# An attention layer and a routed expert layer on one core: smaller last tiles, expert tables in pieces, earlier first products, weights in pieces

## The chip, the cores and the metric

The kernel runs on one core of one Trainium2 chip. The metric is the device time of one execution in microseconds, as the median of several runs. The engines are called as in the profile: PE (TensorE), PEld (its weight loads), DVE (VectorE), ACT (ScalarE), POOL (GpSimd), SP (SyncE).

## The reference

The input is x, 16 sequences of 512 tokens with 128 features, in 32-bit floats. What is computed:

```python
def _layernorm(x, axis=-1, eps=1e-05): ...
# attention, 16 heads of 8
scores = jnp.einsum('bhqd,bhkd->bhqk', Q, K) / jnp.sqrt(jnp.float32(dk))
probs = jax.nn.softmax(scores, axis=-1)
intervened = probs.at[:, :, :, 0].set(0.0)
intervened = intervened / jnp.clip(intervened.sum(axis=-1, keepdims=True), 1e-09, None)
combined = probs + LAMBDA * (intervened - probs)      # LAMBDA = 0.5
x = _layernorm(x + (combined @ V) @ Wo.T + bo)
# experts: each token goes to the best two of 8, weighed by phi_routing
for e in range(E):
    h = jax.nn.silu(x @ w1[e].T) * (x @ w3[e].T)      # 128 -> 512
    out = out + wte[:, e:e + 1] * (h @ w2[e].T)       # 512 -> 128
x = _layernorm(x + out)
```

## The kernel before

**Attention.** The work is cut into 64 units (16 sequences of 4 groups of 4 heads), and the whole program into periods of one unit, from -12 to 63, each of 8 steps. Every engine runs the same list of periods by itself, and semaphores tie them together. In period p the scores and exponentials of unit p are computed (lines 472 and 635), the row maxima of unit p+2 (461 and 769), and the products with the values of unit p-1 (484). The products for q, k and v of a later sequence, the output product and the routing products stand at fixed steps between them: the table `BEHIND` at line 240. So that q and k can be multiplied in bf16, each is split into three bf16 parts by `split_qk` on POOL (1096 to 1109: copy, subtract, copy, subtract). SP stores the parts in DRAM (`store_parts`, 316) and `load_qk` (324) loads them into four large buffers, `regions`, in six transfers for each unit.

**Start.** SP issues wq, wk, bq, bk, then the first xT, then wv, gate, four pieces of wo, bv and bo (300 to 309). All twelve weights count on one semaphore, and PE (527), ACT (624) wait for all of it ahead of their first work. DVE first fills the rows 64 to 127 of two regions with ones (752), then sets the constants of its own (753 to 760).

**Routing.** When a sequence is through the first layer norm, DVE works out its two experts and the places of its rows in six parts (`route`, 828), POOL counts (`count_rows`, 1177) and scatters 1,024 rows of 132 words to `rows_d` in DRAM, expert by expert (`scatter`, 1192: two choices of four indirect DMAs). A row holds the token, its number and its weight.

**Experts.** `rows_d` is read in tiles of 256 rows of one expert. There are 71 (`TILES`, 43): 64 full ones' worth of rows and up to 7 more because each expert's last tile is part empty. The first 45 (`FIRST`) come from the first 13 sequences (`ROUTED`), which are scattered when the tiles start. The tables of a tile's expert and first row are worked out on DVE in two lots (`first_tables` at 941, and `rest_by_expert`, `rest_by_tile` at tiles 11 and 12). What is left of attention and routing for the last three sequences is done among the first 13 tiles: the functions `tail` of DVE and POOL, `TAIL_RING` of PE and ACT.

A tile t runs so. SP loads its rows into one of 6 buffers (410 to 413; the buffer is free when the result of tile t-6 was scattered). PE transposes (`tile_in`, 547), ACT copies the transposed rows out (706) and the two expert weights into fixed buffers (`copy_weights`, 695, two copies of 128x512 whatever the tile's size). PE makes up (560), ACT its silu (721), PE lin (569), DVE their product (1037), PE down (585), DVE scales by the row's weight (1031), POOL adds the rows to `x1_d` or `y_d` in DRAM in turn, 128 rows for each indirect DMA (1272). The order on PE is the loop at line 600:

```python
tile_up(t); beside(t, 0); tile_in(t + 1); tile_down(t - 1); tile_lin(t); beside(t, 1)
```

The sums up and lin have one buffer each: `tile_up` waits for the silu of the tile before, `tile_lin` for the product of the tile before. The weights W1 and W3 (2 MB each) are loaded in one transfer each in period 61 (362 to 365) into regions that attention no longer needs, and W2 ahead of the row load of tile 6 (397 to 399).

**Order at the seam.** SP loads the rows of tile 0 when 13 sequences are scattered (392 to 394). POOL scatters sequence 13 behind the row load of tile 0 (1240 to 1242, `pool.wait_ge(*rows_in(0))`), sequence 14 at tiles 6 and 7, sequence 15 at tiles 11 and 12.

**Final stage.** Five buffers, the sum of `x1_d` and `y_d` on PE (617), statistics on DVE, the factors on POOL, the normalisation on ACT.

## Time and profile before

| what | value |
|---|---|
| median of 3 runs | 1364.8 us (1364.0 to 1367.9) |
| the profiled execution's own time | 1357.14 us |
| its span from the first to the last instruction | 1355.4 us |
| mean granted clock of TensorE | 0.981 of 2.4 GHz |
| busy: PE, DVE, ACT, POOL | 1272.2, 941.3, 822.7, 725.4 us |
| attention, up to the first up product of the experts | 0 to 891.4 us |
| tiles, from the first to the last up product | 891.4 to 1294.1 us |
| final stage, from its first load | 1309.6 to the end |

How the rows are read. In the windows a row gives the stretch and its length, then the busy time of PE, PEld, DVE, ACT and POOL with their instructions in brackets, the granted clock of TensorE (1.00 is 2.4 GHz, 0.50 is 1.2 GHz), the busy share of the DMA engines and GB/s. In a timeline a row gives the start, how long it took, engine, line and operation, what it writes and reads, the count, and in brackets how long the engine idled before it and what released it; "SPq" is the queue of SP, and several merged operations are one row. In the chain of waits a row gives the start, the length and the work; it is the chain that is followed back from the last instruction. Buffers that are used twice have the name of the first owner: `probs_sb` are also the tile's silu, product and result, `values_sb` are also the rows of a tile, `k_parts_sb` the transposed rows, `xT_sb`, `full_q_sb` and `full_k_sb` the copied expert weights. fp32 matmuls are two records each.

### The profile page before, as it was taken

How to read it: one execution, taken by the hardware profiler on the slowest of the kernel's cores; microseconds unless marked ns; L12 is line 12 of the kernel's file. 1: busy time of each engine (PE TensorE's matmuls, PEld its weight loads, DVE VectorE, ACT ScalarE, POOL GpSimd, SP SyncE). 2: the span in 40 equal slices, each digit the busy share in tenths (PEclk: the TensorE clock that was granted, in tenths of full speed). 3: DMA queues.
4: the chain of work that ended last, by engine and by line, in shares of the span. 5: the costliest groups of instructions: out<-in, count | busy, mean ns of one | idle time of the engine just before them, and what ended most of it. 6: DMA issues, size and time to landing. Idle time of an engine off the chain costs nothing.

```text
span 1355.4 us, 22134 instructions
## 1 busy us (share of the span) xinstructions
PE 1272.2 (94%) x7214; PEld 657.1 (48%) x7214; DVE 941.3 (69%) x1560; ACT 822.7 (61%) x1587; POOL 725.4 (54%) x913
## 2 busy tenths in 40 slices
PE   2799999999999999999999999998899999999967
PEld 1133333333333333333333333257789999999942
DVE  6788898898899898988988999833533333333324
ACT  1277777777777777777777777763434444444416
POOL 4324254474474564654644733546775555555547
PEclk8699999999999999999999999999999999999979
DMA  3322323233323323233232231443344333333327
GB/s 102 121 87 67 94 70 98 80 94 93 95 82 94 109 71 105 84 94 91 88 97 81 84 95 33 152 131 54 59 73 69 53 51 48 48 49 46 43 94 279
DMA packets 111888, 117.18 MB, mean 86 GB/s; under 512 B 17440, under 2 KB 91680, under 8 KB 111392
## 3 DMA queue, kind: packets, MB, share of 16 engines
q1 hardware_dynamic: 86960, 97.62, 23.5%
q0 software_dynamic: 24816, 18.15, 9.2%
q8 instruction: 60, 0.98, 0.3%
q14 instruction: 52, 0.43, 0.1%
HBM read 70.81 MB, written 45.29 MB: 86 GB/s over the span
## 4 chain that ended last, share of the span: by engine, by line
PE 72%; DVE 16%; issue 4%; POOL 3%; DMA 2%; ACT 1%; SPq 1%; another core or an unknown queue 0%; POOLq 0%; ACTq 0%; DVEq 0%
PE acc_ps L484 15%; PE ring_ps L472 13%; PE mx_ps L461 12%; DVE rowmax_sb L769 10%; PE ring_ps L585 8%; PE mx_ps L569 8%; PE mx_ps L560 8%; PE ring_ps L504 1%; PE ring_ps L501 1%; PE ring_ps L499 1%; PE ring_ps L509 1%; POOL x_d L1272 1%; PE ring_ps L518 1%; PE ring_ps L550 1%; DVE TN_sb L778 1%
## 5 line engine op out<-in xcount | busy, mean ns | idle before, releaser
L769 DVE TENSOR_REDUCE rowmax_sb<-mx_ps 128x2 f32<-128x1024 f32 x512 | 607.0, 1213 | 88.3 <-PE mx_ps L461 82.9
L635 ACT ACTIVATE probs_sb<-ring_ps 128x512 f32<-128x512 f32 x1024 | 558.7, 598 | 103.9 <-PE ring_ps L472 88.8
L472 PE MATMUL ring_ps<-region_sb 74*128 74x512 bf16 x1024 | 356.8, 381 | 3.7 <-ACT prefix_sb L671 2.1
L461 PE MATMUL mx_ps<-region_sb 72*128 72x512 bf16 x1024 | 310.3, 385 | 11.1 <-DVE rowmax_sb L769 5.2
L484 PE MATMUL acc_ps<-probs_sb,values_sb 128*32 128x512 f32 x2048 | 272.6, 605 | 5.4 <-DVE TN_sb L778 5.4
L472 PEld LDWEIGHTS ring_ps<-region_sb 74*128 74x128 bf16 x1024 | 100.9, 99 | 234.7 <-ACT probs_sb L635 131.8
L702 ACT ACTIVATE xT_sb<-region_sb 128x512 f32 x71 | 44.8, 630 | 207.4 <-PE mx_ps L569 187.8
L1091 POOL CAST negmax_parts_sb<-negmax_sb 16x128 bf16<-16x128 f32 x64 | 17.9, 280 | 274.9 <-ACT negmax_sb L641 274.9
L1272 POOL DMA_INDIRECT x_d<-probs_sb,values_sb x72 | 111.9, 1554 | 87.4 <-DVE probs_sb L1031 66.5
L461 PEld LDWEIGHTS mx_ps<-region_sb 72*128 72x128 bf16 x1024 | 95.7, 99 | 123.7 <-DVE rowmax_sb L769 36.1
L1031 DVE TENSOR_SCALAR probs_sb<-ring_ps,values_sb 128x128 f32<-128x128 f32 x142 | 43.2, 346 | 159.6 <-PE ring_ps L585 146.0
L1196 POOL DMA_INDIRECT rows_d<-sent_sb,pos_sb x128 | 126.2, 986 | 48.4 <-issue 43.7
L585 PE MATMUL ring_ps<-region_sb,probs_sb 128*128 x1136 | 139.4, 276 | 10.1 <-DVE probs_sb L1037 9.9
L1272 POOL DMA_INDIRECT y_d<-probs_sb,values_sb x70 | 108.7, 1553 | 72.9 <-DVE probs_sb L1031 59.8
L1037 DVE TENSOR_TENSOR probs_sb<-mx_ps,probs_sb 128x1024 f32<-128x1024 f32 x71 | 86.9, 1224 | 79.9 <-PE mx_ps L569 76.1
L560 PE MATMUL mx_ps<-k_parts_sb,xT_sb 128*128 128x256 f32 x568 | 135.9, 383 | 2.8 <-issue 2.8
L585 PEld LDWEIGHTS ring_ps<-region_sb,probs_sb 128*128 128x128 f32 x1136 | 132.4, 192 | 12.6 <-issue 12.4
L560 PEld LDWEIGHTS mx_ps<-k_parts_sb,xT_sb 128*128 128x128 f32 x568 | 108.3, 191 | 18.6 <-issue 3.9
L484 PEld LDWEIGHTS acc_ps<-probs_sb,values_sb 128*32 128x32 f32 x2048 | 40.5, 108 | 113.3 <-issue 94.4
L721 ACT ACTIVATE probs_sb<-mx_ps 128x1024 f32<-128x1024 f32 x71 | 72.6, 1022 | 9.2 <-PE mx_ps L560 6.6
L569 PE MATMUL mx_ps<-k_parts_sb,full_q_sb 128*128 128x256 f32 x288 | 68.1, 379 | 0.0
L569 PE MATMUL mx_ps<-k_parts_sb,full_k_sb 128*128 128x256 f32 x280 | 66.2, 379 | 0.0
(150 smaller groups left out, 1206.0 us busy)
## 6 DMA issues: line engine op xcount, KB each, us to landing
region_sb<-parts_d SPq DMA_DIRECT2D x384, 96.0 KB
values_sb<-rows_d SPq DMA_DIRECT2D x71, 132.0 KB
parts_d<-q_parts_sb SPq DMA_DIRECT2D x16, 384.0 KB, 2.6
parts_d<-k_parts_sb SPq DMA_DIRECT2D x16, 384.0 KB, 2.9
xT_sb<-xT SPq DMA_DIRECT2D x16, 256.0 KB, 3.1
x_sb<-x SPq DMA_DIRECT2D x16, 256.0 KB
x_d<-xn_sb SPq DMA_DIRECT2D x16, 256.0 KB
y_d<-padrow_sb SPq DMA_DIRECT2D x16, 256.0 KB
```

What stands on the lines that cost most here:

```text
L461: last = nc.tensor.matmul(mx_ps[n % 2][:, i, :], QS[b % 2][0:KR, h, P * c:P * (c + 1)], KS[b % 2][0:KR, h, :], start=True, stop=True)
L472: nc.tensor.matmul(bank, KS[b % 2][0:KR + MR, h, P * c:P * (c + 1)], QS[b % 2][0:KR + MR, h, :], start=True, stop=True).then_inc(s_ring_re ...
L484: last = nc.tensor.matmul(acc_ps[VW * j:VW * (j + 1), 0, :], VE[b % 2][:, c, HG * g + j, :], PT[u % 2][:, j, c, :], start=(c == 0), stop=( ...
L560: last = nc.tensor.matmul(up_ps[:, c, :], W1T[t % 2][:, P * c:P * (c + 1)], XGT[t % 2], start=True, stop=True)
L569: last = nc.tensor.matmul(lin_ps[:, c, :], W3T[t % 2][:, P * c:P * (c + 1)], XGT[t % 2], start=True, stop=True)
L585: last = nc.tensor.matmul(y_ps[:, at:at + D], HH[t % 2][:, c, P * w:P * (w + 1)], W2[:, bass.ds(expert + c * D, D)], start=(c == 0), stop= ...
L635: nc.scalar.activation(PT[u % 2][:, i // QC, i % QC, :], ring_bank("st", u, i), ACT.Exp, scale=SCALE).then_inc(s_ring_done, 1)
L721: nc.scalar.activation(SG[t % 2], up_ps, ACT.Silu).then_inc(s_silu, 1)
L769: V.tensor_reduce(rowmax[u % 2][:, 2 * k:2 * k + 2], mx_ps[n % 2][:, :, :], axis=AXX, op=ALU.max, negate=True).then_inc(s_mx_done, 1)
L1037: V.tensor_tensor(HH[t % 2], lin_ps, SG[t % 2], ALU.mult).then_inc(s_h, 1)
L1196: G.indirect_dma_start(rows_d, bass.IndirectOffsetOnAxis(ap=pos[b % 2][:, s, c:c + 1], axis=0), XE[b % 2][:, c, s, :], None).then_inc(s_sc ...
L1272: G.indirect_dma_start((x1_d, y_d)[t % 2], bass.IndirectOffsetOnAxis(ap=XG[t % RING][:, w, D:D + 1].bitcast(i32), axis=0), YO[t % YRING][: ...
```

## The change

1. A tile is full (256 rows) or half (128 rows). 57 full ones come first, then 21 halves, 78 in all. Every operation of a half tile has half its columns, but for the two weight copies. A half tile has one scatter-add instead of two.
2. The tables are worked out for the full tiles among the rows known at first (45), for 12 more full ones, and for the halves, the latter two in six pieces at tiles 15 to 27. The running sum over experts has three additions instead of seven.
3. POOL scatters sequence 13 in period 63, behind `send_x` of sequence 14, and no longer waits for rows. SP's first row load waits until 14 sequences are scattered. Sequence 14 is scattered in twos at tiles 6 to 9, sequence 15 at tiles 13 to 16. Step 5 of sequence 14's routing moves from tile 3 to behind the layer norm of tile 5, steps 4 and 5 of sequence 15 to tiles 10 and 12.
4. xT of the first sequence is issued first; the first products wait for wq, wk, bq and bk alone; v, the halved wo and the rest wait for the other eight.
5. The first k is split on DVE, beside POOL's split of q. The rows of ones are written as 32-bit words that hold two bf16 ones (64x4096 instead of 64x8192), one region before that split and one behind it, and a unit's load waits for its own region only.
6. W1, W3 and W2 are loaded in quarters, each when the unit that held its place is through: W1 and W3 in periods 57 to 60, W2 in 61 to 63 and ahead of tile 6's rows.

The core of the diff:

```diff
-TILES = 2 * NT // TK + E - 1
+FULL = 2 * NT // TK - (E - 1)
+TILES = FULL + (2 * NT - FULL * TK) // P + E - 1
...
+        def split_done(b, which):
+            return (s_k0_split, 1) if (b, which) == (0, 1) else (s_split, split_no(b, which) + 1)
+        def halves(t):
+            return HALVES if t < FULL else 1
...
+            load_xT(0)
             for dst, src in ((wq_sb, wqT), (wk_sb, wkT), (bq_sb, bq), (bk_sb, bk)):
-                sp.dma_start(dst[:, :], src).then_inc(s_weights, 16)
-            load_xT(0)
+                sp.dma_start(dst[:, :], src).then_inc(s_weights_qk, 16)
...
-                    sp.wait_ge(s_ones, 2)
+                    sp.wait_ge(s_ones, b % 2 + 1)
...
+            def load_weights(u, s_loaded, *weights):
+                sp.wait_ge(s_ring_ready, ring_at["st", u, 15] + 1)
+                words = slice(E * F // NG * (u % NG), E * F // NG * (u % NG + 1))
+                for dst, src in weights:
+                    sp.dma_start(dst[:, words], src[:, words]).then_inc(s_loaded, 16)
...
-                if p == UNITS - NG + 1:
-                    sp.wait_ge(s_ring_ready, ring_at["st", UNITS - NG - 1, 15] + 1)
-                    for dst, src in ((W1, w1T), (W3, w3T)):
-                        sp.dma_start(dst[:, :], src).then_inc(s_w13, 16)
...
+                if UNITS - 2 * NG < p <= UNITS - NG:
+                    load_weights(p - 1, s_w13, (W1, w1T), (W3, w3T))
+                elif p > UNITS - NG:
+                    load_weights(p - 1, s_w2, (W2, w2T))
...
-            sp.wait_ge(s_scattered, SPARE + SENT * ROUTED)
+            sp.wait_ge(s_scattered, SPARE + SENT * (ROUTED + 1))
...
-            pe.wait_ge(s_weights, s_weights_last)
-            pe.wait_ge(s_const, 6)
+            pe.wait_ge(s_weights_qk, s_weights_qk_last)
...
                 for c in range(FC):
-                    last = nc.tensor.matmul(up_ps[:, c, :], W1T[t % 2][:, P * c:P * (c + 1)], XGT[t % 2],
+                    n = P * halves(t)
+                    last = nc.tensor.matmul(up_ps[:, c, 0:n], W1T[t % 2][:, P * c:P * (c + 1)], XGT[t % 2][:, 0:n],
                                             start=True, stop=True)
...
-            for n in range(2):
-                V.memset(KS[n][64:P, :, :], 1.0).then_inc(s_ones, 1)
-            dve.wait_ge(s_const, 6)
+            two_ones = float(np.array([0x3F803F80], np.uint32).view(np.float32)[0])
+            V.memset(regions[2][64:P, :], two_ones).then_inc(s_ones, 1)
+            dve.wait_ge(s_ring_done, ring_at["k", 0] + 1)
+            exact, parts = full[1], qk_parts[1]
+            V.tensor_copy(parts[:, 0, :], exact[:, :]).then_inc(s_k0_step, 1)
+            dve.wait_ge(s_k0_step, 1)
+            V.tensor_tensor(exact[:, :], exact[:, :], parts[:, 0, :], ALU.subtract).then_inc(s_k0_step, 1)
...
+            V.tensor_tensor(parts[:, 2, :], exact[:, :], parts[:, 1, :], ALU.subtract).then_inc(s_k0_split, 1)
+            V.memset(regions[3][64:P, :], two_ones).then_inc(s_ones, 1)
+            dve.wait_ge(s_const, 1)
...
-                elif t == 3:
-                    route(NB - 2, 5)
...
                 elif t == 5:
                     ln_apply(NB - 1)
+                    route(NB - 2, 5)
...
-                elif t in (9, 10):
-                    route(NB - 1, t - 5)
-                elif t == 11:
+                elif t == 10:
+                    route(NB - 1, 4)
+                elif t == 12:
+                    route(NB - 1, 5)
+                elif t == 13:
                     V.tensor_copy(end_i[:, :], offs[0:1, QC, :]).then_inc(s_ends, 1)
+                elif t == 15:
+                    full_by_expert()
...
                 if g == 3:
                     if is_seq(b - 1):
                         send_x(b - 1)
+                    if b == NB - 1:
+                        for s in range(2):
+                            scatter(b - 2, s)
...
                 if t == 0:
-                    pool.wait_ge(*rows_in(0))
-                    for s in range(2):
-                        scatter(b - 2, s)
                     add_bo(b)
...
-                elif t in (6, 7):
-                    scatter(b - 1, t - 6)
-                elif t == 9:
-                    count_rows(b)
-                elif t in (11, 12):
-                    scatter(b, t - 11)
+                elif t in (6, 7, 8, 9):
+                    if t == 9:
+                        count_rows(b)
+                    scatter(b - 1, (t - 6) // 2, range(t % 2 * 2, t % 2 * 2 + 2))
+                elif t in (13, 14, 15, 16):
+                    scatter(b, (t - 13) // 2, range((t - 13) % 2 * 2, (t - 13) % 2 * 2 + 2))
...
-                for w in range(HALVES):
+                for w in range(halves(t)):
                     G.indirect_dma_start((x1_d, y_d)[t % 2], bass.IndirectOffsetOnAxis(
```

## Rows read from the trace of the kernel before

**Rows 1.** Windows: the first tile and 100 us of steady tiles.

```profile
892.00:896.00 4.00, 4.00 (x19) 2.13 (x21) 1.09 (x6) 2.08 (x3) 3.38 (x4) 0.58 0.94 365
1150.00:1250.00 100.00, 100.00 (x622) 91.39 (x622) 33.64 (x56) 43.34 (x72) 55.76 (x36) 1.00 0.35 47
```

**Rows 2.** Chain of waits over one steady tile: start us, us, what.

```profile
1201.22 1.73 PE mx_ps L560 x8
...
1203.16 1.79 PE ring_ps L585 x16
1204.95 1.73 PE mx_ps L569 x8
```

**Rows 3.** Chain of waits of the first 60 us, the pieces that hold it.

```profile
8.23 5.51 DMA bo_sb<-bo
...
14.18 2.06 PE ring_ps L499 x2
...
24.50 2.83 DMA parts_d<-k_parts_sb
...
45.16 4.47 DMA xT_sb<-xT
```

**Rows 4.** Timeline of the first 45 us: start us, us long, engine line op.

```profile
2.58 6.88 DVE L752 MEMSET region_sb<- 64x8192 bf16 x1 [2.58 <-issue]
2.67 0.43 SPq L298 DMA_DIRECT2D xT_sb<-xT  x1
...
17.97 0.69 ACT L650 ACTIVATE full_k_sb<-ring_ps,bk_sb 128x512 f32<-128x512 f32 x1 [1.02 <-PE ring_ps L501]
...
19.63 1.15 POOL L1109 TENSOR_TENSOR q_parts_sb<-full_q_sb,q_parts_sb 128x512 bf16<-128x512 f32 x1
...
35.02 11.68 DVE L769 TENSOR_REDUCE rowmax_sb<-mx_ps 128x2 f32<-128x1024 f32 x10 [8.19 <-PE mx_ps L461]
```

**Rows 5.** Line 298 in the first 10 us.

```profile
DMA to landing us min/median/max: 2.9/2.9/2.9
```

**Rows 6.** Timeline from the last attention unit to the first tile.

```profile
881.06 0.25 POOL L1175 TENSOR_SCALAR dest_sb<-dest_sb 128x8 f32<-128x8 f32 x1
...
882.65 6.77 SPq L412 DMA_DIRECT2D values_sb<-rows_d  x6
...
885.18 1.09 POOL L1196 DMA_INDIRECT rows_d<-sent_sb,pos_sb  x1 [3.87 <-DMA values_sb<-rows_d]
...
891.44 3.35 PE L560 MATMUL mx_ps<-k_parts_sb,xT_sb 128*128 128x256 f32 x8 [2.78 <-issue]
...
894.19 0.95 POOL L1196 DMA_INDIRECT rows_d<-sent_sb,pos_sb  x1 [0.30 <-issue]
```

**Rows 7.** Timeline of a steady tile on ACT, DVE and POOL.

```profile
1201.32 1.22 DVE L1037 TENSOR_TENSOR probs_sb<-mx_ps,probs_sb 128x1024 f32<-128x1024 f32 x1 [1.19 <-PE mx_ps L569]
...
1201.87 0.63 ACT L702 ACTIVATE xT_sb<-region_sb 128x512 f32 x1 [3.05 <-PE mx_ps L569]
...
1202.98 1.02 ACT L721 ACTIVATE probs_sb<-mx_ps 128x1024 f32<-128x1024 f32 x1
...
1203.90 0.38 ACT L706 ACTIVATE k_parts_sb<-ring_ps 128x256 f32<-128x256 f32 x1
...
1206.36 1.55 POOL L1272 DMA_INDIRECT x_d<-probs_sb,values_sb  x1 [2.06 <-DVE probs_sb L1031]
```

**Rows 8.** Timeline of two tiles late behind counts, and a late signal.

```profile
920.06 0.19 DVE L888 TENSOR_TENSOR place_sb<-prefix_sb,offs_sb 128x32 f32<-128x32 f32 x1 [4.44 <-POOL offs_sb L1190]
...
922.55 2.05 PE L585 MATMUL ring_ps<-region_sb,probs_sb 128*128 x16 [1.08 <-DVE probs_sb L1037]
...
961.83 0.61 DVE L1031 TENSOR_SCALAR probs_sb<-ring_ps,values_sb 128x128 f32<-128x128 f32 x2 [4.38 <-remote]
```

**Rows 9.** Chain of waits from the last tile to the final stage.

```profile
1294.05 1.73 PE mx_ps L560 x8
...
1306.78 2.71 DMA x_d<-probs_sb,values_sb
```

More of the change, by code:

```diff
@@ L280, in rows_out @@
         def rows_out(t):
-            return s_y_out[t % YRING], 16 * HALVES * (t // YRING + 1)
+            return s_y_out[t % YRING], 16 * sum(halves(n) for n in range(t % YRING, t + 1, YRING))
         def is_tile(t):
@@ L568, in tile_lin @@
                 for c in range(FC):
-                    last = nc.tensor.matmul(lin_ps[:, c, :], W3T[t % 2][:, P * c:P * (c + 1)], XGT[t % 2],
+                    n = P * halves(t)
+                    last = nc.tensor.matmul(lin_ps[:, c, 0:n], W3T[t % 2][:, P * c:P * (c + 1)], XGT[t % 2][:, 0:n],
                                             start=True, stop=True)
@@ L581, in tile_down @@
                     pe.wait_ge(s_y, t - 1)
-                for w in range(HALVES):
+                for w in range(halves(t)):
                     at = TK * (t % 2) + D * w
@@ L623, in _ @@
         def _(act):
[L624 to L625 removed]
+            act.wait_ge(s_weights_qk, s_weights_qk_last)
             def ring_bank(*what):
@@ L901, in tb, with whole_tiles, tile_places @@
                 dve.wait_ge(s_tab, step_of_tab[0])
[L903 removed]
+            cnt, tiles, cum, taken, move, upto, start = (tabc[:, n, :] for n in range(7))
             tile_no, expert, row0, woff = (tab[:, n, :] for n in range(4))
[L906 removed]
+            def whole_tiles(n, rows):
                 tb(V.tensor_copy(tabi[:, :], n))
[L908 removed]
+                tb(V.tensor_scalar(tabi[:, :], tabi[:, :], rows.bit_length() - 1, None, ALU.logical_shift_right))
                 tb(V.tensor_copy(tiles, tabi[:, :]))
             def running_sum():
[L912 to L916 removed]
+                of, into = padded[:, 0, :], padded[:, 1, :]
+                tb(V.tensor_copy(of[:, E:2 * E], tiles))
+                for shift in (1, 2):
+                    tb(V.tensor_tensor(into[:, E:2 * E], of[:, E:2 * E], of[:, E - shift:2 * E - shift], ALU.add))
+                    of, into = into, of
+                tb(V.tensor_tensor(cum, of[:, E:2 * E], of[:, E - 4:2 * E - 4], ALU.add))
+            def tile_places(first, last):
                 ge, gn = tile_by_expert(first, last)
@@ L924, in by_tile @@
                     return x.unsqueeze(1).to_broadcast([1, last - first, E])
+                tb(V.tensor_scalar(move, tiles, -1.0, None, ALU.mult))
+                tb(V.tensor_tensor(move, move, start, ALU.subtract))
+                tb(V.tensor_tensor(move[:, 0:E - 1], move[:, 0:E - 1], start[:, 1:E], ALU.add))
                 tb(V.tensor_tensor(ge, tile_no[:, 0:last - first].unsqueeze(2).to_broadcast([1, last - first, E]),
@@ L930, in tile_table, with tile_rows @@
                 tb(V.tensor_reduce(no, gn, axis=AXX, op=ALU.add))
+            def tile_rows(first, last, rows):
+                which = slice(first, last)
+                no = tab[:, 4, 0:last - first]
                 tb(V.tensor_tensor(no, tile_no[:, 0:last - first], no, ALU.add))
-                if first > 0:
-                    tb(V.tensor_tensor(no, no, taken[:, 0:1].to_broadcast([1, last - first]), ALU.add))
+                tb(V.tensor_tensor(no, no, start[:, 0:1].to_broadcast([1, last - first]), ALU.add))
                 tb(V.tensor_scalar(row0[:, which], expert[:, which], float(REGION), None, ALU.mult))
-                tb(V.scalar_tensor_tensor(out=row0[:, which], in0=no, scalar=float(TK), in1=row0[:, which],
+                tb(V.scalar_tensor_tensor(out=row0[:, which], in0=no, scalar=float(rows), in1=row0[:, which],
                                           op0=ALU.mult, op1=ALU.add))
@@ L1028, in _ @@
                         dve.wait_ge(*rows_out(t - 1 - YRING))
-                    for w in range(HALVES):
+                    for w in range(halves(t - 1)):
                         at = TK * ((t - 1) % 2) + D * w
@@ L1270, in _ @@
                     pool.wait_ge(*rows_out(t - 2))
-                for w in range(HALVES):
+                for w in range(halves(t)):
                     G.indirect_dma_start((x1_d, y_d)[t % 2], bass.IndirectOffsetOnAxis(
```

123 lines of the change are left out of this document (74 added, 49 removed).

## The prediction

> **What bounds the kernel now.** I read the profile in five steps. First the busy shares and the 40 slices: TensorE is at nine tenths nearly everywhere, so the question is which waits remain at the seams and what TensorE does in the expert stage. Second, the windows: in 100 us of steady tiles PE is busy for all 100, at full clock, while ACT has 43, DVE 34 and POOL 56 [rows 1]. Only fewer PE columns make this stage shorter. Third, the chain of waits over one steady tile: up 1.73 us, two transposes in a gap of 0.21, down 1.79, lin 1.73, 5.46 us in all, with nothing but PE in it [rows 2]. Fourth, the chain of the first 60 us. The first product starts at 14.18, when the last weight (bo) has landed, though it uses neither bo, wo nor wv. Behind it lie product, bias, both splits one after the other on POOL, the store of k at 24.50 and its landing, then a row of loads issued by SP; the load of the third xT (45.16) still ends a wait [rows 3]. So this stretch is a chain, and what leaves it shifts all of attention. Fifth, the seam to the experts and the end [rows 6, 8, 9]. The first up starts at 891.44 and the last at 1294.05 [rows 6, 9]: 402.6 us for 70 tiles, where 70 x 5.46 is 382.2. Some 20 us are lost among the first sixteen tiles.
>
> **Part 1, the first products.** Before, the xT load was issued fifth, at 2.67, and landed 2.9 later [rows 4, 5], at 5.6. Now xT goes first and the four small loads end in that place; I take the same 5.6 for the last of them, so the first product starts 14.18 - 5.6 = 8.6 us earlier. Lower bound of the gain 7.5 (four loads behind a 256 KB one), upper 9.2. The k split moves from POOL, where it stood behind the q split (ended 20.78) [rows 4], to DVE. k leaves ACT at 18.66, that is 4.5 after the product's start [rows 4]. Four DVE operations on 128x512: the only row of such work is 1.22 us for 1024 elements [rows 7], so 0.65 each, 2.6 together. k can be stored 7.1 after the product's start instead of 24.50 - 14.18 = 10.3: 3.2 us more. The q split (6.6 after the start) stays just ahead of it. I give back 0.5 us because the remaining weights (landed 13.74 [rows 3]) now share the queues with the stores. Sum: -11.3 us; ends -8 (DVE and POOL slow each other) and -13. Cover: the DVE memset of 6.88 writes words instead of halves, half as many elements, 3.4 us; the second one now follows the split, until 16.2. The constants took from 18.0 to 26.8 on DVE [rows 4], 8.8 us, so they end near 25.0, while the first maxima could start at 35.02 - 11.3 = 23.7. They are 1.3 us late, but ten of them ended at 46.7 [rows 4] and the next waited for xT until 49.63 [rows 3]: 2.9 us of cover. The late constants cost nothing; without the cover they would cost 1.3.
>
> **Part 2, expert weights in pieces.** The same bytes are issued in the last seven periods behind the move of the row maxima; each period lasts 10 us or more. In the trace nothing waits for W1 or W3, and the first down follows the second up without a gap. I take 0, between -1 (a lighter W2 load; the DMA share was 0.94 under it [rows 1]) and +3 (the loads of q, k and maxima queue behind a piece).
>
> **Part 3, the new wait ahead of the first tile.** This is the part that speaks against the change. SP issued the first row load at 882.65, when 13 sequences were scattered; the fourteenth was scattered from 885.18 on, after that load had landed 2.5 us later, and its eight scatters took until 895.1 [rows 6], a pitch of 1.29 us. Now POOL begins them when it has sent the fifteenth sequence, at 881.3, and SP waits for all of them ahead of its first load. Last scatter done: 881.3 + 0.4 + 7 x 1.29 + 0.95 = 891.7. Landing: the nearest row has 2.71 for a scatter-add [rows 9]; a plain one I take at 2.0. Register read and issue 0.5, load 2.5, transposes and copy 0.9: the first up starts at 897.6 instead of 891.44, +6.2 us. Queued behind SP's wait are the other five row loads (1.35 each) and the last quarter of W2; the second down needs it only some 9 us later. PE has nothing else in its order. The clock: behind a wait of 2.78 us the granted clock was 0.58 over 892 to 896, the 1.2 GHz level for most of it, and the first up took 3.35 instead of 1.73 [rows 1, 6, 2]. After a wait of 9 us I expect at least the same and half as much again: +0.8. Sum +7.0, ends +3 and +10. The Trainium skill ("TensorE: Matmul & The Clock Gate", section "HAM oscillation") says that a wait for DMA lets the gate fall so that the following work starts cold; it speaks against this part, and this trace agrees for the short wait with the 3.35 us.
>
> **Part 4, the tail of attention among the tiles.** The part of routing that needs POOL's counts now stands three or more tiles behind them. DVE waited 4.44 us for the counts and down stood 1.08 [rows 8]; a second such place, three sequences' scatters later, cost as much. Against that, POOL does its work in nearly the same order and route step 5 now lies behind the layer norm. Three signals of PE came late while scatters were in flight (one DVE wait of 4.38 with an unknown releaser [rows 8]); scatters in twos may or may not calm that. Tables in pieces of at most some ten small operations fit in DVE's 66 idle us of 100 [rows 1]: 0. Sum -3, ends 0 and -8.
>
> **Part 5, 57 full and 21 half tiles for 71.** No pass is lost: eight experts leave less than one full tile each, so 57 full ones always exist. Down already has 128 columns: 1.79 / 16 = 0.112 per matmul, against 1.73 / 8 = 0.216 for 256 columns [rows 2]. A half tile is 24 x 0.112 + 0.11 = 2.80 us of PE. ACT doesn't halve: its weight copies begin 0.65 after the last lin and take 1.11, then half of silu 0.51 and of the copy 0.25: 2.52 [rows 7]. DVE: 0.1 + 0.65 until down may start, under the 1.0 of up and transpose. POOL: one scatter-add of 1.55 and about 0.8 of lead [rows 7]. PE stays the bound with 0.3 us to spare; I take 2.85. So 14 x 5.46 = 76.4 is exchanged for 21 x 2.85 = 59.9: -16.5 us. Ends: -17.6 (2.80) and -5 (3.4: ACT's silu and copy don't shrink, 3.06, and 0.3 of semaphores).
>
> **Part 6, the last tile.** Behind the last lin half of the multiply (-0.6), of down (-0.9), of the scaling (-0.3) and one scatter-add with its lead (-1.85) go: -3.6; ends -2.5 and -4.5. The final stage is unchanged.
>
> **Sum.** -11.3 + 0 + 7.0 - 3.0 - 16.5 - 3.6 = -27.4. The profiled execution took 1357.1: 1329.7. The median of the runs shown, 1364.8, lies 7.7 above it; I keep that distance: 1337. A measurement of this kernel can tell some 0.3% (4 us) from no change.
>
> **Rivals.**
> *Half tiles keep their fixed parts.* A slot falls to 3.6 us instead of 2.85, since the copies, semaphores and the single-buffered sums stay as they are. For it: ACT is only 0.3 us shorter than PE. Against: DVE and ACT idle for more than half of a full tile. 21 x 3.6 = 75.6: part 5 gives 0.8, the total -11.7, 1353. Chance 0.16. The Trainium skill ("VectorE: DVE Perf Modes", section on the TRN2 errata) has SBUF-source operations pay a fixed latency each and advises 512 elements or more; that speaks for this rival. The slots here keep 512 elements except the copy of 128, and no row of before shows that one.
> *The seam costs little and the late signals go.* Part 3 at +3, part 4 at -8: -36.4, 1328. Chance 0.12.
> *Slower: the ring of row buffers.* A tile's rows are loaded when the scatter of six tiles before has landed; if load, scatter-add and landing keep the full tile's time, the half tiles go at the pace of that loop. By rows it is 3 (read, issue, load) + 2 slots and 1.25 + 0.8 + 1.55 + 2.71 = 15 us for six, 2.5 per tile, under 2.85. It decides from 4.2 per tile: (76.4 + 10.9) / 21. At 4.6 the time is +9.3, 1374. Chance 0.05.
>
> **How the numbers follow.** The forecast has 0.67: 1337, its own range 1326 to 1347. Rivals 0.16, 0.12, 0.05. The range from 1320 to 1355 holds forecast, both faster rivals and the ends of parts 1 and 3; the slower rival is left out. Faster by over 4 us: 0.93; within: 0.03; slower: 0.04.
>
> **What would show it.** First product near 5.6 and k stored near 12.7; first maxima around 25; first up near 897.6 with the clock at half behind it; half tiles of 2.85 in the chain with PE alone; the last scatter issued 3.6 nearer to the last lin. Wrong would be: ACT or DVE in the chain of the half tiles, first up before 893, a wait for xT that doesn't move.

## The result and the profile after

Four executions of the changed kernel took 1332.5 to 1347.9 us, median 1344.5; the kernel before took 1364.4 beside it (1351.8 to 1367.9). The ratio is 0.9868, with an interval from 0.9828 to 0.9908: 18 us faster, between 12.6 and 23.5. The forecast was 1337 us and 27.4 us faster. Executions of one kernel spread by some 10 us or more, so the runs below are compared by their ratios and milestones.

The profiled execution took 1345.6 us, span 1343.7, against a span of 1355.4: 11.7 us shorter. Where these went, from one milestone to the next (the forecast of +7.0 has 6.2 for the wait up to the first up and 0.8 for the lower clock behind it):

| stretch | before | after | difference | forecast |
|---|---|---|---|---|
| start to last exponential of attention | 887.5 | 889.55 | +2.05 | -11.3 |
| from there to the first up | 3.94 | 11.46 | +7.5 | +7.0 |
| first up to the 58th up | 331.5 | 323.4 | -8.1 | -3.0 |
| 14 full tiles, or 21 half ones | 76.45 | 64.1 | -12.4 | -16.5 |
| last slot's end to first final load | 10.3 | 6.6 | -3.7 | -3.6 |
| final stage | 45.8 | 48.7 | +2.9 | 0 |

**The start.** The chain of waits of the changed kernel answers to [rows 3] (start us, us, what):

```profile
2.67 2.41 DMA bk_sb<-bk
5.12 2.09 PE ring_ps L521 x2
7.28 1.28 ACT L677
8.58 0.69 ACT full_q_sb L677
9.27 0.59 ACT full_k_sb L677
...
14.19 3.46 DMA parts_d<-k_parts_sb
17.72 0.70 SPq L354
...
35.48 4.96 DMA xT_sb<-xT
```

The first product starts at 5.12 instead of 14.18, k is stored at 14.19 instead of 24.50, SP issues the first of the row of q and k loads at 17.72 instead of 27.40, and xT at 35.48 instead of 45.16: from the loads on the chain lies 9.7 us earlier. Between 17.72 and 35.48 nothing but SP's own issuing holds it, some 0.7 us for each of 24 loads and 0.45 for each of two stores. The timeline of the two splits, to be read beside [rows 4]:

```profile
9.34 0.61 POOL L1177 CAST q_parts_sb<-full_q_sb 128x512 bf16<-128x512 f32 x1 [3.63 <-ACT full_q_sb L677]
...
10.04 1.28 POOL L1179 TENSOR_TENSOR full_q_sb<-full_q_sb,q_parts_sb 128x512 f32<-128x512 f32 x1
10.34 1.52 DVE L789 TENSOR_TENSOR full_k_sb<-full_k_sb,k_parts_sb 128x512 f32<-128x512 f32 x1
...
12.64 1.52 DVE L793 TENSOR_TENSOR k_parts_sb<-full_k_sb,k_parts_sb 128x512 bf16<-128x512 f32 x1
...
27.64 9.42 DVE L811 TENSOR_REDUCE rowmax_sb<-mx_ps 128x2 f32<-128x1024 f32 x8
```

The subtractions took 1.52 us each on DVE, the whole split 4.3. Both end 0.54 us behind the subtraction of POOL that was under way when they began (11.32 and 13.62 on POOL, 11.86 and 14.16 on DVE). PE began the products for the first maxima at 24.20; DVE takes the maxima at 27.64, 0.03 behind the last of its constants.

Then the 9.7 us are lost again, and the windows show to what (us, busy time and count of PE, PEld, DVE, ACT, POOL, granted clock, DMA share, GB/s):

```profile
30.00:50.00 20.00, 16.31 (x31) 3.81 (x32) 14.57 (x14) 1.64 (x3) 1.81 (x5) 0.50 0.48 149
50.00:100.00 50.00, 49.96 (x196) 16.37 (x195) 34.38 (x31) 30.62 (x59) 12.00 (x19) 0.71 0.20 62
```

The same two windows of the kernel before:

```profile
30.00:50.00 20.00, 11.72 (x33) 3.27 (x32) 11.68 (x10) 2.24 (x4) 10.00 (x13) 0.67 0.52 163
50.00:100.00 50.00, 48.27 (x224) 15.02 (x225) 40.66 (x36) 33.35 (x64) 12.02 (x19) 0.91 0.27 82
```

PE is busy for nearly all of the 50 us in both (49.96, and 48.27 before), but at a granted clock of 0.71 instead of 0.91 it got through 196 matmuls instead of 224. TensorE had 1.2 GHz, half of 2.4, from 27.8 to 79.0 here, and before from 21.5 to 31.7 and from 38.6 to 59.1. Unit 2's maxima start at 52.0 (before 61.0), unit 4's at 84.6 (82.5), unit 12's at 188.1 (186.0).

**The seam.** POOL's and PE's timeline, which answer to [rows 6]:

```profile
885.13 1.09 POOL L1270 DMA_INDIRECT rows_d<-sent_sb,pos_sb  x1 [0.46 <-issue]
...
894.13 0.96 POOL L1270 DMA_INDIRECT rows_d<-sent_sb,pos_sb  x1 [0.30 <-issue]
```

```profile
899.82 0.66 PE L576 MATMUL ring_ps<-ident_sb,values_sb 128*128 128x128 f32 x2 [9.47 <-DMA values_sb<-rows_d]
901.01 2.50 PE L587 MATMUL mx_ps<-k_parts_sb,xT_sb 128*128 128x256 f32 x5 [0.53 <-ACT k_parts_sb L736]
```

SP issues nothing more from 885.2 until the last of the eight scatters has landed, and issues the first row load at 897.42. PE waits 9.47 us.

**The half tiles.** The chain of one of them, beside [rows 2]:

```profile
1252.85 0.89 PE mx_ps L587 x8
1253.74 0.11 PE ring_ps L576
1253.85 1.09 PE ring_ps L613 x8
1254.94 0.89 PE mx_ps L597 x8
```

That is up, transpose, down and lin: 2.98 us, PE alone. Down has the same count of columns as up and lin and takes 0.2 more.

### The profile page after: what moved, and what is told of

It reads as the page before. It is cut to its first block, busy times and chain, and to the rows that moved or that the text cites. A ratio compares the mean times of both kernels' runs of the same rounds, so it can differ in the third digit from the quotient of the medians.

```text
span 1343.7 us, 22455 instructions
## 1 busy us (share of the span) xinstructions
PE 1274.6 (95%) x7263; PEld 654.0 (49%) x7263; DVE 940.4 (70%) x1591; ACT 830.0 (62%) x1615; POOL 712.2 (53%) x902
## 4 chain that ended last, share of the span: by engine, by line
PE 71%; DVE 20%; issue 2%; DMA 2%; POOL 2%; SPq 2%; ACT 0%; DVEq 0%; POOLq 0%; ACTq 0%
PE acc_ps L506 13%; DVE rowmax_sb L811 12%; PE mx_ps L483 12%; PE ring_ps L494 11%; PE ring_ps L613 9%; PE mx_ps L587 8%; PE mx_ps L597 8%; DVE TN_sb L820 2%; PE mx_ps L645 1%; PE ring_ps L529 1%; PE ring_ps L523 1%; PE ring_ps L521 1%; PE ring_ps L576 1%; PE ring_ps L545 1%; DVE stats_sb L843 1%
## 5 line engine op out<-in xcount | busy, mean ns | idle before, releaser
L494 PE MATMUL ring_ps<-region_sb 74*128 74x512 bf16 x1024 | 361.5, 388 | 1.5 <-ACT probs_sb L662 1.4
L483 PE MATMUL mx_ps<-region_sb 72*128 72x512 bf16 x1024 | 317.8, 393 | 11.5 <-DVE rowmax_sb L811 8.7
L731 ACT ACTIVATE xT_sb<-region_sb 128x512 f32 x78 | 49.1, 630 | 188.1 <-PE mx_ps L597 186.8
L1346 POOL DMA_INDIRECT x_d<-probs_sb,values_sb x68 | 106.1, 1561 | 89.6 <-DVE probs_sb L1103 64.8
L1270 POOL DMA_INDIRECT rows_d<-sent_sb,pos_sb x128 | 126.4, 987 | 48.1 <-issue 47.2
L1110 DVE TENSOR_TENSOR probs_sb<-mx_ps,probs_sb 128x1024 f32<-128x1024 f32 (+1 forms) x78 | 84.3, 1080 | 91.5 <-PE mx_ps L597 91.5
L587 PE MATMUL mx_ps<-k_parts_sb,xT_sb 128*128 128x256 f32 (+1 forms) x624 | 132.2, 355 | 0.5 <-ACT k_parts_sb L736 0.5
L613 PEld LDWEIGHTS ring_ps<-region_sb,probs_sb 128*128 128x128 f32 x1080 | 127.9, 193 | 7.8 <-issue 7.7
L752 ACT ACTIVATE probs_sb<-mx_ps 128x1024 f32<-128x1024 f32 (+1 forms) x78 | 70.4, 903 | 4.6 <-PE mx_ps L587 4.6
L597 PE MATMUL mx_ps<-k_parts_sb,full_q_sb 128*128 128x256 f32 (+1 forms) x312 | 65.4, 353 | 0.0
L597 PE MATMUL mx_ps<-k_parts_sb,full_k_sb 128*128 128x256 f32 (+1 forms) x312 | 65.0, 351 | 0.0
```

Of the source, the lines that this page charges most:

```text
L483: last = nc.tensor.matmul(mx_ps[n % 2][:, i, :], QS[b % 2][0:KR, h, P * c:P * (c + 1)], KS[b % 2][0:KR, h, :], start=True, stop=True)
L494: nc.tensor.matmul(bank, KS[b % 2][0:KR + MR, h, P * c:P * (c + 1)], QS[b % 2][0:KR + MR, h, :], start=True, stop=True).then_inc(s_ring_re ...
L587: last = nc.tensor.matmul(up_ps[:, c, 0:n], W1T[t % 2][:, P * c:P * (c + 1)], XGT[t % 2][:, 0:n], start=True, stop=True)
L597: last = nc.tensor.matmul(lin_ps[:, c, 0:n], W3T[t % 2][:, P * c:P * (c + 1)], XGT[t % 2][:, 0:n], start=True, stop=True)
L613: last = nc.tensor.matmul(y_ps[:, at:at + D], HH[t % 2][:, c, P * w:P * (w + 1)], W2[:, bass.ds(expert + c * D, D)], start=(c == 0), stop= ...
L752: nc.scalar.activation(SG[t % 2][:, :, 0:n], up_ps[:, :, 0:n], ACT.Silu).then_inc(s_silu, 1)
```

## The experiments

Ratios are to the kernel before, timed on the same chip beside each. The milestone "unit 12" is the start of its first maxima: 188.1 us in the profile after.

**The old start.** The loads of weights in their old order, the first products waiting for all twelve, k split on POOL; everything else as changed.

```diff
-            load_xT(0)
             for dst, src in ((wq_sb, wqT), (wk_sb, wkT), (bq_sb, bq), (bk_sb, bk)):
...
+            load_xT(0)
...
             pe.wait_ge(s_weights_qk, s_weights_qk_last)
+            pe.wait_ge(s_weights, s_weights_last)
...
-            V.tensor_copy(parts[:, 0, :], exact[:, :]).then_inc(s_k0_step, 1)
...
-                    if is_seq(b + 2) and b + 2 > 0:
+                    if is_seq(b + 2):
```

> The changed kernel with the old start: the small loads ahead of xT, all twelve weights waited for, the first k split on POOL behind q. Theory (the clock took the gain): the first product starts near 14 and the first maxima near 36 again, some 9 us later, but TensorE's granted clock is back at 2.4 GHz some 20 us sooner than in the changed kernel (59 instead of 79), so the last exponential of attention is where it was, within 3 us, and the time is that of the changed kernel within 4 us. Rival (the gain is real and the changed kernel's profile was unlucky): 9 to 11 us slower than the changed kernel. A second rival (the late constants on DVE hold the first units): the same time as the theory, but with the clock as in the changed kernel.

Measured: median 1349.8 of ten, 0.9941 [0.9908, 0.9975], 0.73% above the changed kernel's ratio (10 us; the two intervals touch). In its profile the first product starts at 13.26 and the first maxima at 35.4; the clock was at half from 19.9 to 33.5 and from 36.9 to 81.3, and unit 12 starts at 194.5, 6.4 later than in the profile after. The theory missed: the clock didn't come back sooner (81.3, not 59), and the time isn't the same. The rival's 9 to 11 us fit. So the new start is worth about what the chain says, some 6 to 10 us, and the loss in the profile after isn't its doing alone.

**Filler.** 27 matmuls more (54 records) in the first 42 us, in places where PE would wait; they multiply what is there, and nobody reads their sums.

```diff
+            def filler(count, rhs):
+                for _ in range(count):
+                    nc.tensor.matmul(acc_ps[:, 0, 0:rhs.shape[-1]], wk_sb[:, :], rhs, start=True, stop=True)
...
+                if (name, b) == ("q", 1):
+                    filler(10, xT_sb[0][:, :])
+                elif (name, b) == ("q", 2):
+                    filler(4, xT_sb[1][:, :])
...
+                        if p == -2 and k == 0:
+                            filler(5, xT_sb[1][:, :])
                         maxima(p + 2, k)
+                        if p == -2:
+                            filler(1, xT_sb[1][:, 0:256])
```

> The changed kernel with extra matmuls on PE between the first products and the first units, into a bank that nothing reads before it is started anew: ten of 512 columns ahead of the second q, five ahead of the first maxima, four ahead of the third q, one of 256 columns behind each step of the first maxima. The output is unchanged. Theory (the half clock from 27.8 to 79.0 us takes the gain of the start): the clock stays at or near 2.4 GHz through the first units, unit 3's maxima come less than 13 us behind unit 2's, the last exponential comes at 874 to 880 instead of 889.6, the time is 9 to 15 us below the changed kernel's. Rival (loads and DVE hold the first units whatever the clock): no gain, or up to 5 us slower by the extra work.

Measured: median 1332.8 of six, 0.9834 [0.9796, 0.9871]. Windows of this kernel:

```profile
30.00:50.00 20.00, 17.21 (x55) 7.30 (x54) 16.12 (x15) 2.35 (x5) 1.57 (x4) 0.91 0.48 155
50.00:100.00 50.00, 49.26 (x261) 15.64 (x260) 42.18 (x39) 39.55 (x78) 12.71 (x21) 1.00 0.23 72
```

261 matmuls in the 50 us instead of 196; unit 4 at 71.5 instead of 84.6, unit 12 at 175.0 instead of 188.1. The last exponential comes at 874.6, in the range that the theory gave. So 13 us of the profiled execution were the clock's. But the interval of the ratio overlaps the changed kernel's, so the timed executions don't show that the filler gains.

**Own semaphore.** Sequence 13's scatters count on a semaphore of their own, and SP's first row load waits for 13 sequences again; the waits that need the fourteenth name the new one.

```diff
+        s_scattered_13 = sem("scattered_13")
...
-            sp.wait_ge(s_scattered, SPARE + SENT * (ROUTED + 1))
+            wait_scattered(sp, ROUTED)
...
-                                         XE[b % 2][:, c, s, :], None).then_inc(s_scattered, 16)
+                                         XE[b % 2][:, c, s, :], None)\
+                     .then_inc(s_scattered_13 if b == ROUTED else s_scattered, 16)
```

> The changed kernel with a semaphore of its own for the scatters of sequence 13, so that SP's first row load waits for 13 sequences again while POOL scatters sequence 13 beside it. Theory (the count waits for a sequence that the first tiles don't need): the first row load is issued near 885 instead of 897.4, first up between 891 and 894 instead of 901.0, 7 to 10 us below the changed kernel. Rival (the loads stand behind the scatters' traffic or late row tables): under 4 us.

Measured: median 1328.6 of six, 0.9797 [0.9754, 0.984], 0.71% below the changed kernel's ratio (10 us; the intervals overlap a little). SP's and PE's timeline:

```profile
876.00 6.68 SPq L441 DMA_DIRECT2D values_sb<-rows_d  x6
...
879.73 0.20 PEld L583 LDWEIGHTS ring_ps<-ident_sb,values_sb 128*128 128x128 f32 x2 [0.84 <-issue]
...
881.25 1.99 PE L594 MATMUL mx_ps<-k_parts_sb,xT_sb 128*128 128x256 f32 x8 [1.07 <-ACT k_parts_sb L743]
```

From the last exponential (879.01) to the first up it is 2.24 us instead of 11.46, and the first up takes 1.99 instead of 3.78, with no stretch of the clock at half behind the seam. Up to here the gain is 9.2 us, and the next seventeen tiles are no longer for it (103.2 against 105.1). The theory holds in its difference; its milestones (first up at 891 to 894) took attention's end from the profile after, and here it lies 10.5 earlier. The program's first 180 us are those of the changed kernel, and yet unit 12 starts at 176.5, with 1.2 GHz from 12.6 to 22.8 and from 26.2 to 50.1.

**All tiles full.** 71 tiles of 256 tokens with everything else of the change.

```diff
-TILES = FULL + (2 * NT - FULL * TK) // P + E - 1
+TILES = 2 * NT // TK + E - 1
...
-            return HALVES if t < FULL else 1
+            return HALVES
```

> The changed kernel with 71 full tiles (14 in place of the 21 halves), tables in the same pieces. By the two profiles the half tiles took 64.1 us for 76.4 and the end behind the last slot 6.6 for 10.3: theory 16 us slower than the changed kernel. Rival (part of the saving is the earlier relief of other queues, or a luckier execution): under 10 us.

Measured: median 1355.6 of ten, 0.9989 [0.996, 1.0018]. From the 58th up to the first final load it is 86.0 us, where the half tiles take 70.6: 15.4, as the theory had it. Without the half tiles the rest of the change is worth nothing that can be measured (between 2 us slower and 5 us faster), although by the profiles start, seam, tail and final stage sum to some 8 us less than before (-10 + 7.5 - 8.1 + 2.9) where the clock behind the start takes one of its shorter courses. The mean granted clock of its ten executions is lower, 0.970 in the median for 0.977 of the kernel before beside them. That fits a loss to the clock in the timed executions too; it isn't shown further. Its final stage takes 48.6 us too.

**The changed kernel again**, beside the next three.

> The changed kernel itself once more, unchanged, beside the others on one chip, for a base and to see how its executions spread. Theory (the granted clock in the first 100 us has two courses, and an execution takes one or the other): the executions fall into two groups some 8 to 12 us apart, the slower one with a mean granted clock lower by 0.008 or more; this profile reaches unit 12's maxima either near 176 or near 188 us. Rival (the spread is noise of the whole program): no gap between groups, and no tie to the clock.

Measured: median 1345.7 of six (1341.7 to 1352.4), 0.9863 [0.9814, 0.9912]. Unit 12 starts at 182.0, with 1.2 GHz from 27.4 to 44.5 and from 51.3 to 68.4: a third course of the clock, of the same instructions. The theory of two courses missed: the six don't fall into two groups (five lie between 1341.7 and 1347.6), and the slowest, 1352.4, had a mean clock of 0.968, where four of the others had 0.966 to 0.970.

**Three repairs at once.** The own semaphore; DVE's product in two operations, each tied to half of lin and half of down; and one activation of a single column ahead of ACT's first wait, so that the function table is loaded there.

```diff
-                pe.wait_ge(s_h, t + 1)
+                pe.wait_ge(s_h, 2 * t + 1)
...
+                        if (w, c) == (0, 2):
+                            pe.wait_ge(s_h, 2 * t + 2)
...
-                    V.tensor_tensor(HH[t % 2][:, :, 0:n], lin_ps[:, :, 0:n], SG[t % 2][:, :, 0:n], ALU.mult)\
-                     .then_inc(s_h, 1)
+                    for i in range(2):
+                        dve.wait_ge(s_lin, 2 * t + i + 1)
+                        cs = slice(2 * i, 2 * i + 2)
+                        V.tensor_tensor(HH[t % 2][:, cs, 0:n], lin_ps[:, cs, 0:n], SG[t % 2][:, cs, 0:n], ALU.mult)\
+                         .then_inc(s_h, 1)
...
+            act.wait_ge(s_pool_const, 1)
+            nc.scalar.activation(first_use[:, :], ones[:, 0:1], ACT.Identity)
             act.wait_ge(s_weights_qk, s_weights_qk_last)
```

> The kernel with the semaphore of its own for sequence 13, and in addition DVE's product of a tile in two operations (columns c 0 and 1, then 2 and 3), each tied to its half of lin and of down, and a first activation on ACT ahead of its wait for the weights, so that the function table is loaded early. Theory (in a half tile down waits for the product, and its first weight load isn't hidden: 0.2 us per half tile): half slots of 2.79 to 2.85 us instead of 2.98, full slots 5.46 as before; the table load of 1.28 leaves the start, k is stored 1.3 us earlier. Together 4 to 5.5 us below the kernel with the semaphore alone, at like clock. Rival (the half slot is bound by the 2.52 us of ACT and the semaphores): half slots stay at 2.95 or more.

Measured: median 1324.4 of six, 0.9711 [0.966, 0.9761], the best of all: 1.5% below the changed kernel beside it. Four of the six took 1323.3 to 1324.9 us at a mean clock of 0.979 to 0.983, two 1334.0 and 1335.4 at 0.968 and 0.971. The chain of a half tile:

```profile
1256.48 0.11 PE ring_ps L584
1256.59 0.89 PE ring_ps L624 x8
1257.48 0.89 PE mx_ps L605 x8
1258.38 0.89 PE mx_ps L595 x8
```

Down takes 0.89, the slot 2.79 instead of 2.98, as the theory had it. The table's load no longer stands in the chain: ACT took k 0.35 earlier (8.81 for 9.16), q 1.4 earlier, and k is stored at 13.11 instead of 14.19. PE begins the products for the first maxima 1.1 earlier, but DVE's constants hold the maxima until 27.05, only 0.6 earlier. Two of DVE's operations on k, now beside other operations of POOL:

```profile
10.09 0.98 DVE L802 TENSOR_TENSOR full_k_sb<-full_k_sb,k_parts_sb 128x512 f32<-128x512 f32 x1
11.10 1.26 DVE L804 CAST k_parts_sb<-full_k_sb 128x512 bf16<-128x512 f32 x1
```

The profile holds one of the longer courses of the clock (half from 23.4 to 74.6). Its seam is 5.8 us, not the 2.24 of the version with the semaphore alone, for ACT got the signal for the first tile's rows late, from a sender that the trace doesn't name, while scatters were in flight:

```profile
897.04 0.38 ACT L749 ACTIVATE k_parts_sb<-ring_ps 128x256 f32<-128x256 f32 x1 [3.76 <-remote]
```

**Scatters in fours.**

```diff
-                elif t in (6, 7, 8, 9):
...
+                elif t in (6, 7):
+                    scatter(b - 1, t - 6)
...
+                elif t in (13, 14):
+                    scatter(b, t - 13)
```

> The changed kernel with the scatters of sequences 14 and 15 in fours at tiles 6, 7, 13 and 14 instead of in twos at eight tiles. Theory (the scatters in bursts of four on POOL push the scatter-adds back, and late signals come with them): from the first up to the 18th takes 109 us or more instead of 105.1, 3 to 7 us slower than the changed kernel. Rival (what went is the wait for POOL's counts on DVE alone): 105 to 107 us, time within 2 us of the changed kernel.

Measured: median 1345.4 of four, 0.9872 [0.9804, 0.994]. The first seventeen slots take 108.8 us where the profile after has 105.1 and the changed kernel again 104.7. Totals of waits over this stretch (engine line waited for: us in total, times, longest), first of the kernel before, then of this one; the changed kernel has no such line:

```profile
DVE probs_sb L1031 <- remote: 13.6, 3, 5.0
```

```profile
DVE probs_sb L1103 <- remote: 7.4, 2, 4.1
```

Of the tail's gain about 4 us belong to the scatters in twos, and the late signals came back with the bursts of four, as the theory had it. In the median these 4 us don't show under the spread of the clock, so the time that the theory gave isn't borne out.

**Weights whole.** W1 and W3 in one transfer each in period 61, W2 in one ahead of tile 6's rows.

```diff
-                if UNITS - 2 * NG < p <= UNITS - NG:
-                    load_weights(p - 1, s_w13, (W1, w1T), (W3, w3T))
...
+                        for dst, src in ((W1, w1T), (W3, w3T)):
+                            sp.dma_start(dst[:, :], src).then_inc(s_w13, 16)
```

> The changed kernel with W1 and W3 loaded whole in period 61 and W2 whole ahead of tile 6's rows, as before. Theory (the pieces hide what was hidden already): last exponential and first up within 1 us of the changed kernel at like clock, the second down not late since it comes 11 us behind the first up; time within 2 us. Rival (the 2 MB of W2 fall on the first tiles' rows): the first tiles 3 to 6 us longer, 3 us or more slower.

Measured: median 1340.6 of four, 0.9833 [0.9768, 0.9897]; from the last exponential to the first up 11.55 us, from there to the 18th up 104.9. The pieces are worth nothing that shows, as the theory had it.

**Three repairs and filler.** The union of those two edits, as in their diffs.

> The kernel with the semaphore of its own, the product in two operations and the early function table, and in addition the extra matmuls of the earlier run ahead of the first units. Theory (the extra matmuls keep the clock at 2.4 GHz, and only the slower half of the executions gains): no execution in the slower group; the ratio to the kernel before 0.963 to 0.968, against 0.9711 without the extra matmuls, the first up between 875 and 881. Rival (the extra work costs what the clock gives): 0.970 or more.

Measured: median 1336.4 of six (1325.6 to 1344.9), 0.9726 [0.9678, 0.9773]: no better than without the filler, so the theory missed. Unit 12 starts at 179.2, with 1.2 GHz from 48.4 to 65.5, behind all of the filler, whose last matmul starts at 39.2. Keeping PE busier in the first 40 us moved the stretch; it didn't remove it. The seam is 6.35 us here, again with a late signal to ACT (3.8).

**q behind k.** POOL's first split waits until DVE has split k.

```diff
+                if (b, which) == (0, 0):
+                    pool.wait_ge(s_k0_split, 1)
```

> The changed kernel with POOL's first split of q held until DVE's first split of k is done, so that the two don't run beside each other. Theory (DVE's subtractions of 128x512 took 1.52 us because POOL worked beside them): they take 0.6 to 0.8 us alone, the copies 0.43, the split 2.5 us in all instead of 4.3, and POOL's second copy 0.61 instead of 0.95. Rival (a subtraction of two SBUF operands takes DVE 1.5 us by itself): 1.5 again. The stores of q and k come later than in the changed kernel, by 1 to 2 us.

Measured: one execution, 1351.5 us. DVE's part of the timeline:

```profile
9.89 0.43 DVE L787 CAST k_parts_sb<-full_k_sb 128x512 bf16<-128x512 f32 x1 [4.69 <-ACT full_k_sb L677]
10.35 0.69 DVE L789 TENSOR_TENSOR full_k_sb<-full_k_sb,k_parts_sb 128x512 f32<-128x512 f32 x1
11.07 0.43 DVE L791 CAST k_parts_sb<-full_k_sb 128x512 bf16<-128x512 f32 x1
11.53 0.69 DVE L793 TENSOR_TENSOR k_parts_sb<-full_k_sb,k_parts_sb 128x512 bf16<-128x512 f32 x1
...
27.41 9.41 DVE L811 TENSOR_REDUCE rowmax_sb<-mx_ps 128x2 f32<-128x1024 f32 x8 [1.88 <-PE mx_ps L483]
```

With POOL still, the four operations take 2.33 us instead of 4.3: the subtractions 0.69 instead of 1.52. But SP stores q ahead of k, q is ready only at 16.05, and k's store goes out at 16.52 instead of 14.19. Here the maxima wait for PE, and begin 0.72 behind its first product for them (26.69). By that the profile after could have had them at 24.9; there they waited for the constants until 27.64. The one delay took the place of the other. One execution can't tell whether the time gains; the order of the two stores would have to change with it, and that wasn't tried.

Together with the two profiles above, the rows give a pattern. Where POOL was at work when DVE began, DVE's subtraction ended 0.54 or 0.55 us behind POOL's operation (at 11.86 and 14.16, and at 11.07 with the three repairs), and DVE's second cast 0.28 or 0.29 behind it: it took 0.72 instead of 0.43 in the profile after and 1.26 with the three repairs. The Trainium skill ("SBUF — State Buffer", section "Who interferes with whom") says that VectorE and GpSimd share one pair of ports under an exclusive lock, that a VectorE instruction with two inputs from SBUF contends with a GpSimd one that reads SBUF, and that a cast can contend as well, in a mode that uses both ports. The trace agrees with both: the subtractions, with two operands from SBUF, went from 0.69 to as much as 1.52, and the cast from 0.43 to 1.26.

## Why the prediction was right, and where it wasn't

The time lay in the range and on the side forecast, 7.5 us above the forecast. By the profiles the parts are off by more: by +13.4, +0.5, -5.1, +4.1 and -0.1 in the order of the table, and by +2.9 for the final stage. In all the profiled execution got 11.7 us shorter for 27.4. That the median lies only 7.5 us off is partly luck: the sum gave 1329.7 for a profiled execution, which took 1345.6, and to it the working added the 7.7 us by which the median of the kernel before lay above its own profiled execution; after the change the median lies 1.1 below it. The half tiles and the last tile carry the gain, as forecast. Step by step:

**Part 1, the start, -11.3.** The chain delivered -9.7 up to the load of xT. The first product starts at 5.12, forecast 5.6. From there to k's store it is 9.07 us for 7.1: 1.7 by a split of 4.3 instead of 2.6, 0.26 by the table. The step that failed is "0.65 each, 2.6 together": alone the four take 2.33, so the price was fair, but it was summed as if POOL's split weren't beside them, and then they take 4.3. Only the lower end, -8, had that. The constants held the maxima up by 2.7 us instead of 1.3, and the cover held: the third q started 9.2 earlier (40.58 for 49.76). The term that is missing altogether, and the largest miss of the sum, is the clock behind the start. Unit 12 starts 2.1 later in the profile after, but 10 earlier (176.0 to 176.5) in four other executions with the same start. All of part 1 hung on PE running at the clock of the kernel before from 30 to 100 us, and no term stood for that.

**Part 2, 0.** Held: whole or in pieces, the tiles take the same.

**Part 3, the seam, +7.0.** Measured +7.5, and +9.2 against the version with its own semaphore. From the end of POOL's preparation to the first up the working had 16.3 us (881.3 to 897.6); the trace has 884.67 to 901.01, 16.3. That preparation ended 1.3 nearer to the last exponential than before (4.9 us for 6.2), which makes the 6.2 forecast up to the first up 7.5. The first up took 3.78 at the lower clock, 0.4 more than before, where that part expected 0.8 in all. The prediction took this wait for a need of the change. It is none: it comes from one counting semaphore, on which "fourteen sequences" can't be told from "thirteen, and some of the fourteenth". Without the wait the tile starts beside the scatters, and then the late signals are back in some executions: ACT's copy started 0.1 us behind the transposes in the profile after and 0.65 with the semaphore of its own, but 2.3 in the kernel before, 4.3 with the three repairs and 4.8 with the filler added to them. So the semaphore is worth 9.2 us in one profile and 5.6 and 5.1 in two.

**Part 4, the tail, -3.** Measured -8.1, its far end. DVE's late signals among these tiles are gone, and the two places behind POOL's counts no longer cost. The rival that joined this to a cheap seam had this half right and the seam wrong.

**Part 5, half tiles, -16.5.** Measured -12.4. Slots of 2.98 for 2.85 make 2.6 of the 4.1 us missing, and the first half slot of 4.41 makes the rest: the down in it is that of the last full tile, 1.79, and waits 0.47 for that tile's product. The working counted 21 equal slots. The step that failed in these is down at 8 x 0.112, or 0.89: it was priced by matmuls whose weights were loaded under the one before. In a half tile DVE's product (0.69 us) ends at 1253.65, when the weights for the transposes are already loaded (to 1253.61), and down's first weights are loaded only from 1253.78 on. So 0.2 us stand in the open. The version with the product in two halves takes that away and has 2.79. The rival with fixed parts, 3.6 a slot, was far off: ACT and DVE never appear in the chain. The lower bound of this part has a slip: the lead, the weight copies, silu and the copy of the rows at full length sum to 3.16, not 3.06, which makes the slot 3.46 and the bound -3.7.

**Part 6, -3.6.** Measured -3.7.

**The final stage, 0.** Measured +2.9, and 47.2 to 49.9 us in every version of the changed kernel, 71 full tiles among them. So it doesn't come from the half tiles. 2.0 us of it stand behind the last store. SP saw that store landed 0.82 us before the end in the kernel before and 2.87 in the profile after. What still runs in between is a drain, POOL's last instruction but for semaphores, which ends 0.23 us before the end. The drains of both profiles, first before, then after (engine, operation, count: shortest, median, longest in ns, first and last start in us):

```profile
L71 POOLq DRAIN  x1: 902/902/902, 1350.7 to 1350.7; - x1
```

```profile
L72 POOLq DRAIN  x1: 6455/6455/6455, 1337.1 to 1337.1; - x1
```

It takes 6.46 to 7.03 us in all eleven profiles of versions of the changed kernel. Which part of the change makes it longer stays open, as does the other 0.9 us, which lies ahead of the last store.

**The slower rival** didn't come: no slot waits for rows.

## What to carry to other kernels

When DMAs are moved ahead of a wait on a counting semaphore, give them a semaphore of their own: here that one wait cost 5 to 9 us, where the whole change brought 18. Where a step is halved, ask which waits lay under its length, and cut the producer in pieces too: beside a 0.89 us step another 0.2 us came into the open. And when a change starts TensorE earlier, look at the granted clock in the first busy stretch of more than one execution before the gain, or the loss, is put down to the chain.

## What the runs showed of the hardware

**The clock's course isn't fixed by the program.** Six profiled executions have the same first 180 us of instructions: own semaphore, all tiles full, fours, weights whole, the changed kernel again, and the profile after. In this order unit 12 starts at 176.5, 176.2, 176.1, 176.0, 182.0 and 188.1. In the first 100 us TensorE was at 1.2 GHz for 34.1 us in the first of these, for 34.1 too in the fifth and for 51.2 in the last. Between the first and the fifth it mattered where the stretches lay. In the last, PE was busy nearly all of the time: 49.96 of the 50 us from 50 to 100. The timed executions spread as the clock does: of the ten with the old start five took 1341.8 to 1346.9 us at a mean clock of 0.975 to 0.981, five 1352.7 to 1356.4 at 0.961 to 0.965. What decides between the courses wasn't found; filler shortened the stretch in one profile (3.4 us) and moved it in the other (17.1 us), but brought nothing that the ratios can tell.

The Trainium skill ("TensorE: Matmul & The Clock Gate", the caveats at the end of the section "Seeing it yourself") warns that the records of the gate are not fully reliable and that it has been seen stuck at a low level, K=1/4, for 50 us and more. The trace agrees for the length, 51.2 us, and shows the level of one half; that the level is real is borne out by the 196 matmuls in 50 us of a busy PE where another profile has 261.

**DVE and POOL on SBUF.** A subtraction of 128x512 took 0.69 us on DVE alone and 0.98 to 1.52 beside POOL, a cast 0.43 alone and up to 1.26; POOL's own subtraction took 1.15 alone and 1.21 to 1.47 beside DVE. Work moved from POOL to DVE to run beside POOL's rest gained only part of its length.

**Late signals beside scatters.** DVE got the end of down late three times in the kernel before (13.6 us in all) and twice with scatters in fours (7.4), and never in the ten profiles with scatters in twos. ACT stood still for the first tile's transposed rows for 1.6, 3.8 and 3.8 us in three of the four profiles in which that tile started beside the scatters of sequence 13. What delays them the traces don't show.
